# Vision-transformer block on one core: values carried per token tile through DRAM, q/k/v products nine tiles late, and the attention pair turned by full-width products

## The reference

```
x  = layernorm(patches) @ W + bias            # 64 x 36 x 768 -> 256
h  = concat(cls, layernorm(x) + position)     # 64 x 37 x 256 = 2368 token rows
q, k, v = split(layernorm(h) @ Wqkv)          # 16 heads of width 16
q, k = rotate(q), rotate(k)
h += softmax(q k^T / 4) v @ Wout
h += bitlinear(gelu(bitlinear(layernorm(h), W1)), W2)
```

## Time and profile before

| | us |
|---|---|
| median of three runs | 387.02 |
| lowest, highest | 383.44, 388.23 |
| profiled execution | 389.49 |
| its span in the profile | 387.7 |

### The profile page before, as it was taken

The page is one execution under the profiler, slowest core; times in us unless marked ns, Lnnn a source line. Parts: engine busy times, 40 slices in busy tenths (PEclk is TensorE's granted clock), DMA queues, the critical chain, the costliest instruction groups (busy, mean ns, idle before and its releaser), DMA issues.

```text
span 387.7 us, 9782 instructions
## 1 busy us (share of the span) xinstructions
PE 328.3 (85%) x3548; PEld 255.5 (66%) x3548; DVE 276.0 (71%) x680; ACT 219.3 (57%) x398; POOL 160.4 (41%) x329
## 2 busy tenths in 40 slices
PE   0648999999999957699889898989886789999874
PEld 0436777777777632588778787878774467777553
DVE  1184577686776675447776767677766899999983
ACT  2344455545577312244555555555553799999993
POOL 4223265464654525324332333323204556656630
PEclk9996999999999997657999999999999999999997
DMA  8997050000000000000000000000000000100101
GB/s 225 311 399 225 9 210 1 2 2 2 0 2 1 0 2 0 2 1 3 2 0 0 0 0 0 0 0 0 0 2 1 1 2 27 43 27 30 43 28 61
DMA packets 9018, 16.10 MB, mean 42 GB/s; under 512 B 944, under 2 KB 5744, under 8 KB 8992
## 3 DMA queue, kind: packets, MB, share of 16 engines
q1 hardware_dynamic: 7936, 13.59, 10.3%
q10 hardware_dynamic: 1056, 2.18, 2.2%
HBM read 13.34 MB, written 2.42 MB: 41 GB/s over the span
## 4 chain that ended last, share of the span: by engine, by line
PE 54%; DVE 18%; ACT 12%; issue 9%; DMA 3%; POOL 3%; ACTq 0%; DVEq 0%; POOLq 0%
PE ps L331 13%; PE ps L407 9%; PE ps L357 7%; DVE sc L811 6%; PE ps L439 4%; DVE ximg L830 4%; PE ps L321 3%; DMA qkT<-in_W 3%; PE ps L415 3%; ACT ximg L1023 2%; PE ps L426 2%; ACT ximg L976 2%; PE ps L314 2%; PE ps L365 2%; PE ps L401 2%
## 5 line engine op out<-in xcount | busy, mean ns | idle before, releaser
L1057 POOL TENSOR_TENSOR rs<-rs,nhalf 128x1 f32<-128x1 f32 (+1 forms) x76 | 41.8, 557 | 120.4 <-DVE rs L622 50.8
L962 ACT ACTIVATE ximg<-ps,byp 128x222 f32<-128x222 f32 x64 | 25.0, 442 | 61.0 <-PE ps L447 54.0
L331 PE MATMUL ps<-w_in,xT 128*128 128x256 f32 (+1 forms) x228 | 55.3, 394 | 2.9 <-ACT xT L896 2.9
L331 PEld LDWEIGHTS ps<-w_in,xT 128*128 128x128 f32 (+1 forms) x228 | 42.8, 195 | 10.5 <-ACT xT L896 4.2
L407 PE MATMUL ps<-hnT,w_v 128*128 (+1 forms) x256 | 38.9, 300 | 12.7 <-ACT ximg L976 7.6
L1101 POOL TENSOR_TENSOR ximg<-qkT,ones_c 128x148 f32<-128x148 f32 x32 | 15.9, 497 | 80.7 <-PE ps L401 79.5
L407 PEld LDWEIGHTS ps<-hnT,w_v 128*128 128x128 f32 x256 | 34.2, 208 | 18.1 <-issue 16.9
L756 DVE TENSOR_TENSOR ximg<-ps,tab 111x512 f32<-111x512 f32 x32 | 22.1, 691 | 31.9 <-PE ps L426 31.9
L357 PE MATMUL ps<-w_qk,hnT 128*128 128x512 f32 (+1 forms) x76 | 37.9, 623 | 6.7 <-DVE qb L673 6.7
L896 ACT ACTIVATE xT<-ps 128x768 f32<-128x768 f32 (+1 forms) x19 | 15.1, 794 | 32.0 <-PE ps L321 32.0
L665 DVE TENSOR_TENSOR qa<-ps,tab 128x512 f32<-128x512 f32 (+1 forms) x19 | 13.1, 689 | 27.8 <-PE ps L314 27.8
(11 more groups left out here) (107 smaller groups left out, 770.5 us busy)
## 6 DMA issues: line engine op xcount, KB each, us to landing
ximg<-in_x SPq DMA_DIRECT2D x18, 384.0 KB, 15.8
out<-ximg SPq DMA_DIRECT2D x18, 128.0 KB, 1.7
ximg<-in_W SPq DMA_DIRECT2D x2, 1024.0 KB, 6.3
wide<-in_rows ACTq DMA_DIRECT2D x1, 768.0 KB, 15.1
w_qk<-in_Wqk SPq DMA_DIRECT2D x1, 512.0 KB, 15.0
qkT<-in_offsets ACTq DMA_DIRECT2D x1, 448.0 KB, 13.3
qkT<-in_W SPq DMA_DIRECT2D x1, 384.0 KB, 6.3
qkT<-in_W ACTq DMA_DIRECT2D x1, 384.0 KB, 11.3
```

The source lines that it names most:

```text
L331: pe.matmul(dst[0:n, :], xT[t % 2][:, k, 0:n], w_in[:, k, :], start=(k == 0), stop=False)
L962: ins = act.activation(vds[u][:, m, :, :].rearrange("p i (r t) -> p i r t", r=3), src, ACT.Identity, bias=b_v[:, m:m + 1])
L1057: pool.tensor_tensor(rs[u][0:n, i:i + 1], rs[u][0:n, i:i + 1], nhalf[0:n, :], ALU.pow).then_inc(S[done], 1)
```

## The change

* **Values.** v is no longer made per pair with the channel in the partition, but per token tile in the patch stage (`value_product`, two products of 256 columns). ACT copies it beside a column of ones per head, SP stores the tile to a DRAM tensor `vsc`, and SP reloads it per pair in the block layout that `attend` needs (`load_values`, two DMAs a pair, four buffers). The four transposes, DVE's `place_values` and ACT's `values_out` per pair fall away. The bias of v goes through Wout once at the start (`out_offset`), and w_o and w_v are loaded earlier.
* **Order of the patch stage.** q, k and v of a tile are formed nine steps after its pixels are turned (LAG = 9, before 4), and q and k are turned at step s-11 (before s-6). So the patch stage has 30 steps where it had 25.
* **Attention.** The scores read q and k from `qkT`; ACT writes both masked copies of k when it empties `turn_qk`, so POOL stages nothing. The probabilities lie at a pitch of 64 and are turned by eight products of a 128-column stationary block with 101 columns of the identity, two PSUM banks (4 and 5) of four; the attended rows are turned by two such products into the same banks. Before these were transposes. `attend` has 16 products of 34 columns (before 12 of up to 51). All steps are written out, without the hardware loop.
* **Ternary weights.** POOL does both matrices during the attention; before DVE did them.

The core of the diff:

```diff
+LAG = 9
+HB = LAG - 2
...
+            def value_product(t):
+                pe.wait_ge(S["h_canvas"], min(t + HB - 1, NT + 1))
+                war(pe, "v_evac", t, 1)
...
+                n = rows(t)
+                for k in range(2):
+                    mm = pe.matmul(ps_v[0:n, :], hnT[t % HB][:, k, 0:n], w_v[:, k, :], start=(k == 0), stop=(k == 1))
+                mm.then_inc(S["v_ready"], 1)
...
-                if live(s - 4, NT + 1):
-                    qk_product(s - 4)
+                if live(s - LAG, NT + 1):
+                    qk_product(s - LAG)
+                    value_product(s - LAG)
                 if live(s - 3, NT + 1):
                     turn_h(s - 3)
...
+            def turn_probs(p, b):
                 pe.wait_ge(S["s_exp"], p + 1)
-                war(pe, "p_evac", p, 1)
-                for g in range(HG - 1):
-                    mm = pe.transpose(ps_pT[0:V3, g, :], pr[u][0:SPAN, V3 * g:V3 * g + V3], ident[0:SPAN, 0:SPAN])
...
+                war(pe, f"p_evac{b}", p, 1)
+                for g in range(4):
+                    at0 = 2 * 64 * (4 * (b - 4) + g)
+                    flat = pr[p % 2][:, :, :].rearrange("p h t -> p (h t)")
+                    mm = pe.matmul(ps[:, b, SPAN * g:SPAN * g + SPAN], flat[:, at0:at0 + 128], ident[:, 0:SPAN],
+                                   start=True, stop=True)
+                mm.then_inc(S[f"p_turned{b}"], 1)
+
+            def turn_out(p, b):
+
+                pe.wait_ge(S["o_norm"], p + 1)
+                pe.wait_ge(S[f"p_evac{b}"], min(p + 2, NP))
+                war(pe, "o_canvas4" if b == 4 else "o_canvas", p, 1)
+                m = b - 4
+                pe.matmul(ps[:, b, O_AT:O_AT + SPAN], at[p % 4][:, 128 * m:128 * m + 128],
+                          ident[:, 0:SPAN], start=True, stop=True).then_inc(S[f"o_turned{b}"], 1)
...
+            def attention_step(s):
+                if live(s, NP):
+                    scores(s)
+                if live(s - 3, NP):
+                    turn_out(s - 3, 5)
+                    turn_out(s - 3, 4)
+                if live(s - 2, NP):
+                    attend(s - 2)
                 if live(s - 1, NP):
...
+                    turn_probs(s - 1, 4)
+                    turn_probs(s - 1, 5)
...
+            def attended_out(p, b):
+                act.wait_ge(S[f"o_turned{b}"], p + 1)
+                act.wait_ge(S[f"p_turned{b}"], min(p + 3, NP))
...
+            def attention_step(s):
+                if live(s - 3, NP):
+                    attended_out(s - 3, 4)
+                    attended_out(s - 3, 5)
+                if live(s - 1, NP):
+                    probs_out(s - 1, 4)
+                    probs_out(s - 1, 5)
                 if live(s, NP):
...
+                    exponentials(s)
```

More of the change, by code:

```diff
@@ L216, in vit_block @@
         ymid = two("ymid", [128, D])
+        hnT = [sb(f"hnT{u}", [128, 2, 128]) for u in range(HB)]
+        vt = two("vt", [128, 2, HC, VW])
         hn = two("hn", [128, D])
@@ L309, in _, with out_offset @@
             pe.wait_ge(S["ld_tab"], 16)
+            def out_offset():
+                pe.wait_ge(S["ld_o"], 16)
+                for k in range(2):
+                    mm = pe.matmul(ps[0:K3, 7, 0:D], bass.AP(byp, 2 * KP + k, [[2 * KP + 2, 128], [0, K3]]),
+                                   w_o[:, k, :], start=(k == 0), stop=(k == 1))
+                mm.then_inc(S["orow"], 1)
             def add_rows(dst, t, which, only=False):
@@ L376, in patch_step, with scores @@
                     turn_pixels(s)
-                if live(s - 4, NT + 1):
-                    qk_product(s - 4)
+                if live(s - LAG, NT + 1):
+                    qk_product(s - LAG)
+                    value_product(s - LAG)
                 if live(s - 3, NT + 1):
                     turn_h(s - 3)
-            for s in range(NT + 2):
+                if s == 0:
+                    out_offset()
+            for s in range(NT + LAG + 1):
                 patch_step(s)
[L385 to L392, removed]
+            def scores(p):
+                pe.wait_ge(S["qk_canvas"], tiles_of(p))
                 war(pe, "s_sub", p, 1)
@@ L430, in attend @@
[L430 to L437, removed]
+                            at0 = PW * p + TOK * i
+                            rhs = bass.AP(qkT, qkT[32 * r:32 * r + 32, 2 + c, at0:at0 + TOK].offset,
+                                          [[6 * COLS, 32], [2 * COLS, 2], [1, TOK]])
@@ new lines, in turn_out, with attend @@
+            def turn_out(p, b):
[5 more added lines that the diff above has]
+                          ident[:, 0:SPAN], start=True, stop=True).then_inc(S[f"o_turned{b}"], 1)
+            def attend(p):
+                pe.wait_ge(S["p_evac4"], p + 1)
+                pe.wait_ge(S["p_evac5"], p + 1)
+                pe.wait_ge(S[f"vb{p % 4}"], 32 * (p // 4 + 1))
+                war(pe, "o_norm", p)
+                for g in range(HC):
@@ L483, in _ @@
+            pe.wait_ge(S["y_mid"], NT + 1)
+            attention_step(0)
+            patch_step(NT + LAG + 1)
+            pe.wait_ge(S["h_ready"], NT + 1)
+            pe.wait_ge(S["v_evac"], NT + 1)
+            attention_step(1)
+            patch_step(NT + LAG + 2)
+            pe.wait_ge(S["a_init"], 2)
+            for s in range(2, NP + 1):
+                attention_step(s)
             pe.wait_ge(S["ld_o"], 16)
@@ L779, in _ @@
-            pieces = ternary(1, w2, w2t)
-            for s in range(5):
-                attention_step(s, s % 2)
-                if s >= 2:
-                    next(pieces)
-            steps(v, attention_step, A_FIRST, A_LAST, NP + 2, begin=5)
+                    soften(s)
+            v.wait_ge(S["p_zero"], 1)
+            attention_step(0)
+            patch_step(NT + LAG + 1)
+            v.wait_ge(S["qk_rot"], NT + 1)
+            v.memset(ps[:, 6, 0:NH * VW], 1.0).then_inc(S["a_init"], 1)
@@ L786, in residual @@
+            attention_step(1)
+            v.wait_ge(S["qk_canvas"], NT + 1)
+            v.memset(ps[:, 7, 0:NH * VW], 1.0).then_inc(S["a_init"], 1)
+            for s in range(2, NP + 3):
+                attention_step(s)
             def residual(t):
@@ L998, in _ @@
+            attention_step(0)
+            patch_step(NT + LAG + 2)
+            for s in range(1, NP + 3):
+                attention_step(s)
             act.preload_act_table(ACT.Gelu)
```

396 lines of the change are left out of this document (177 added, 219 removed).

## The result

The changed kernel takes **409.22 us** (median of 4 runs, 408.97 to 410.75); the kernel before, run beside it on the same chip, 385.43 us (383.44 to 388.23). The ratio is **1.062, 95% interval 1.054 to 1.070**: slower. An execution more than 1.5% above the fastest one of its kernel counts as slow and stands in no ratio here, though it stands in the medians and ranges. The forecast was 404 us in 387 to 414.

What follows compares the result with a forecast made beforehand. PE alone bounds the patch stage and runs nearly gapless in the pairs. Terms +13.4, -6.6, +8.0 and +2.1 give +16.9 us: the profiled 389.49 becomes 406.4, or 404 us on the median's basis; range 387 to 414.

Steps and rivals of the forecast that it cites:

- 1. Patch stage: Start to first scores: added value products and late q/k steps put first scores at 169.0 us, +13.4 us.
- startup: Patch stage start: offset rows wait for w_o and one more DVE addition, +1.3 us until tile 1 is turned.
- 2. The seam: First scores to scores of pair 3: 10.4 us against 16.95 before at the low clock, -6.6 us.
- Rival C: Seam: the clock falls and three or four pairs cost 1.9 us more each; total 411 us, chance 0.24.
- 3. The pairs: Attention: twenty identity passes on a closed PE-ACT loop, period 4.27 us, 28 periods 119.6 against 111.55, +8.0 us.
- the restart terms: Closed loop of a pair: 0.05 us for ACT's start and 0.10 us for PE's restart.
- 4. The drain: Scores of pair 31 to first output projection: 10.9 us against 8.78 before, +2.1 us.
- B: Pairs: passes cost 0.09 us, 0.022 in attend; period 3.6 to 3.9, total 386 to 394, chance 0.23.
- D: Pairs: identity products take one pass like a transpose, 1.07 us less a pair; total 374 us, chance 0.08.
- E: Pairs: reloaded values land later than 16 us; at 20 us each pair waits 1 us more, 432 us, chance 0.02.
- F: Pairs: weight loads hide behind nothing, 1.7 us more a pair, total 451 us, chance 0.01.

Runs made afterwards that it cites:

- e6: The kernel before with only the attention's hardware loop written out, same instructions; 378.59 us, ratio 0.977.
- e3: The changed kernel with LAG = 4 instead of 9, POOL clearing the probability padding ahead of the value buffers; 406.77 us, ratio 1.051.
- e9: The changed kernel with probabilities turned by 64 of the identity's 101 columns from pair 1 on; 488.1, 490.1, 408.7 and 489.1 us.
- e1: The changed kernel with its ten identity products per pair made transposes again; 371.14 us, ratio to before 0.954.
- e5: The changed kernel with the edits of e1, e2 and e3 together; 356.5 us, ratio 0.919.
- e7: e5 with PE's order changed to interleave the two banks and ACT's exponential between its copies of banks 4 and 5; 348.7 us, ratio 0.898.
- e4: The changed kernel with an extra 32-column product ahead of each product that turns probabilities; 601.6, 478.1, 601.5 and 601.1 us.
- e2: The changed kernel with ACT's copies alternating attended rows and probabilities, bank 4 then bank 5; 399.63 us, ratio 1.035.
- e8: The kernel before with only its eight transposes of probabilities and outputs per pair made identity products; 409.18 us, ratio 1.050.

## Why the prediction was right, step by step

| mark, us | before | predicted | measured |
|---|---|---|---|
| first scores | 155.61 | 169.0 | 169.47 |
| first scores to scores of pair 3 | 16.95 | 10.4 | 11.23 |
| 28 periods | 111.55 | 119.6 | 121.74 |
| to the output projection | 8.78 | 10.9 | 11.28 |
| sum against before | | +16.9 | +20.8 |

The forecast of 404 us was 17 above the median of the kernel before; the medians lie 23.8 apart. Of the missing 6.8 us the marks explain 3.9. The rest comes from the basis of the sum, the profiled execution of the kernel before, at 389.49 us the slowest on record: its clock was at the lower level for 21 us behind the first scores, and for 10 in e6's profile. So a part of what the seam gained in the table is the clock of that one execution and not the change.

**1. Patch stage: right, to 0.5 us of a shift of 13.9.** The parts: startup +0.45 (I had 1.3), early steps 4.53, steps with the value product 6.49 and then about 6.9, q/k products in the tail 3.65 apart (I had 3.7), with 0.17 us idle for DVE's rotation. The cost is what PE's own work adds, the value product (0.86 us, 18 times), less what the cleared pauses give, plus the lateness of the q/k/v products: with LAG = 4 (e3) the first scores come 6.5 us earlier.

**2. The seam: the chain was right, the clock was not in it.** Scores of pair 2 came 6.78 us after those of pair 0 (I had 7, though the terms that I listed add up to 6.6). The next pair took 4.45 where I had 3.3: the clock fell to 0.57 for 3.4 us. Rival C came true for one pair. My price for it was too low: I charged 0.168 us a pass at the lower level, by the columns, and it is 0.226 to 0.229, load again (e3, e9). The Trainium skill ("TensorE: Matmul & The Clock Gate", "Part 4: PE-mode transpose") says that transposes do not count as activity for the clock. The traces do not bear this out as an account of the seam. Its low stretch is 3.4 us in the changed kernel and 10.3 in e1, which has transposes; but it is 10.2 in e3, which has products, and 6.8 in e5 and e7, which have transposes. And 60 us of e1's pairs with 20% idle PE and ten transposes each ran at 1.00.

**3. The pairs: the mechanism was right, two sizes were off and nearly cancelled.** A pass with 128 stationary columns costs 0.1225 us (1.96 / 16); I took 0.107 from L387, which has two moving columns, in a range that ended at 0.12. Over 20 passes that is 0.31 us too little, and most of a pass is the load (0.10 with 32 columns in e4, and no gain with 64 in e9), so a narrower moving side would have helped little. `attend` costs 0.0216 a pass with 37 stationary and 34 moving columns; I carried over the 0.032 of 51 moving ones and so charged 0.32 too much. Here the moving columns did count, against what I wrote: 0.0216 to 0.032 is as 34 to 51. That the two errors took each other away is luck. Left over: the restart terms, 0.1 us a pair. The wait ahead of L484, predicted at about 0.75 and released by L1000, is 0.62 and released by L1000; e2 shows that it is the order of ACT's copies.

**4. The drain: right,** 0.4 us longer.

**The rivals.** B (cheap passes) held for `attend` alone and had its opposite in `turn_probs`. D (one pass per identity product) is refuted by the sixteen records of L474 and by e8's ten for five. E (late values) has no row: loads land in 2.0 us, and nothing ahead of L496 is released by a DMA. F (no overlap of load and stream) would have made a pair 1.7 us longer than it is.

What I had not named at all is the split that e6 and e1 show. Step by step from kernel to kernel, the period is 3.91 before, 3.65 with the loop written out (e6), 3.03 with the rest of the change but with transposes (e1), and 4.36 with products in place of the transposes. In this order the steps are worth -0.26, -0.62 and +1.33 us; in another order they could share out otherwise, as e8 shows for the pause. The forecast got the sum by counting passes; it did not say that one part of the change cost 41 us and the rest gained more than 16.

## What to carry to other kernels

- A float32 product with the identity is two passes, a transpose one, and with 128 stationary columns and about 100 moving ones both passes are bound mostly by the load: count passes and stationary columns first. Here the choice decided the sign, 371 against 409 us, with 387 before.
- Where an engine with time to spare has copies for which the bound engine waits, the order of its copies and the order of the bound engine's groups are worth a look for each pair of halves: two reorderings without any change of work took e1's structure from a mean period of 3.03 to 2.59 (e5 and e7; the shorter lag in them does not touch the pairs, see e3).
- A pause put down to "issue" inside a hardware loop is not nothing: writing the loop out saved 0.26 us a pair, 2.3% of the kernel before. It was a wait for another engine that the loop made longer, so look at the neighbouring pairs before calling it the loop's own.

## What the hardware showed that was not expected

**A clock that does not come back under full load.** In e4 and e9 the granted clock fell to 0.50, the 1.2 GHz level, in the seam, and in three of four executions each stayed there through the attention: the profiled one in the rows below, the two others by their times and mean granted clocks (0.715 in e4, 0.766 and 0.769 in e9). e4, and e9, in the windows of their pairs:

```profile
181.00:300.00 119.00, 115.34 (x1139) 108.04 (x1135) 26.27 (x48) 18.39 (x54) 4.29 (x3) 0.50 0.06 12
```

```profile
200.00:300.00 100.00, 94.52 (x1230) 85.72 (x1213) 32.77 (x58) 24.81 (x74) 0.00 (x0) 0.50 0.08 17
```

PE was busy in 115.3 of 119 and in 94.5 of 100 us. The price is 80 us in e9 (488.6 against 408.7) and 123 in e4. In the changed kernel it came back after 3.4 us, in e5 and e7 after 6.8, in e1 and e3 after 10, in the kernel before after 21, with PE busy in 20.1 of the 23 us of the last row. The two kernels that lost it differ from the changed one only in the moving side and the number of products in `turn_probs`; what in that keeps the clock low was not tried and stays open. What is shown is that a busy PE alone does not bring the clock back, and that the same program can go either way.

**The load of 128 stationary columns sets most of a pass, at both levels.** At the full clock a pass takes 0.10 us with 32 moving columns (e4) and 0.1225 with 101. At half it takes 0.226 with 64 (e9) and 0.229 with 101 (e3).
